# Attention made tile by tile: q, k and v of 128 tokens in one group of split fp32 products, used and dropped

## The reference, cut to what matters

```python
q = apply_rope(rmsnorm((x @ Wq + bq).heads, qn_w), pos)          # 16 heads of 128
w = softmax((x @ Wcmp + bcmp) in groups of 4 tokens)
entries = weighted sum of each 4 tokens                            # 512 entries
ck = apply_rope(rmsnorm(entries @ Wk + bk, kn_w), block_ends)
cv = entries @ Wv + bv
sc = where(causal, q @ ck.T / sqrt(128), NEG)
tv, ti = top_k(sc, 8)                                              # 8 entries of 512
ctx_sparse = softmax over those 8 of cv
lk = apply_rope(rmsnorm((x @ Wlk + blk).heads, kn_w), pos)
lv = (x @ Wlv + blv).heads
ctx_local = softmax(q @ lk.T / sqrt(128)) @ lv                    # own and former 128 tokens
out = ((ctx_sparse + ctx_local) / 2).heads_joined @ Wo + bo
x = layernorm(x + out)                                             # then the experts
```

## Time and profile before

| | us |
|---|---|
| median of 3 runs (lowest, highest) | 2773.98 (2771.32, 2775.93) |
| span of the profiled execution, first to last instruction | 2770.1 |
| its PE busy / DVE / ACT / POOL | 2483.0 / 1509.1 / 915.2 / 897.2 |
| preparation (`compress`) | 0 to 60 |
| heads | 60 to 1770 |
| first norm, routing, experts, second norm | 1770 to 2770 |

### The profile page before, as it was taken

One profiled execution on the slowest core, in us unless ns is written; L12 is line 12 of the kernel. 1 busy time (PEld: TensorE's weight loads), 2 busy tenths in 40 slices (PEclk: granted clock), 3 DMA queues, 4 the chain that ended last, 5 costly groups with the idle time before them and its releaser, 6 DMA issues. The chain is left out here.

```text
span 2770.1 us, 43311 instructions
## 1 busy us (share of the span) xinstructions
PE 2483.0 (90%) x14112; PEld 1983.1 (72%) x14113; DVE 1509.1 (54%) x4673; ACT 915.2 (33%) x2231; POOL 897.2 (32%) x969
## 2 busy tenths in 40 slices
PE   6999999999999999999999998599278999988873
PEld 4676876876876876877877877377167999877852
DVE  5566666666666666666666666707023222344357
ACT  2143343343343343343333334332012333333331
POOL 1333233233233233233233232224702110256256
PEclk9999999999999999999999999789688999999986
DMA  4900000000000000000000000101514332446446
GB/s 183 356 1 21 13 1 21 14 1 21 14 1 21 14 1 21 14 1 21 14 1 21 1 1 1 68 0 46 197 44 147 110 112 76 141 161 218 133 132 187
DMA packets 63673, 176.74 MB, mean 64 GB/s; under 512 B 8832, under 2 KB 10368, under 8 KB 63232
## 3 DMA queue, kind: packets, MB, share of 16 engines
q1 hardware_dynamic: 31792, 84.39, 8.7%
q0 software_dynamic: 19456, 69.22, 7.7%
q10 hardware_dynamic: 12240, 20.73, 2.0%
HBM read 107.20 MB, written 67.11 MB: 63 GB/s over the span
## 5 line engine op out<-in xcount | busy, mean ns | idle before, releaser
L448 PE MATMUL bank<-xT,wh 128*128 128x512 f32 x1024 | 468.5, 601 | 1.6 <-PEq L156 1.6
L698 POOL TENSOR_TENSOR prob<-prob,share 128x256 f32<-128x256 f32 (+1 forms) x256 | 153.6, 600 | 818.5 <-DVE share L611 818.5
L448 PEld LDWEIGHTS bank<-xT,wh 128*128 128x128 f32 x1024 | 187.8, 194 | 190.7 <-issue 190.7
L1389 POOL TENSOR_TENSOR ring_lo<-staged,ring_hi 128x1088 fp32r<-128x1088 f32 x51 | 127.9, 2523 | 475.9 <-ACT ring_hi L1348 475.4
L646 ACT COPY probT<-bank 128x128 f32<-128x128 f32 (+3 forms) x256 | 109.1, 426 | 482.2 <-PE bank L490 482.2
L455 PE MATMUL bank<-wh,xT 128*128 128x128 f32 x2048 | 263.4, 275 | 0.0
L606 DVE SCALAR_TENSOR_TENSOR prob<-taken,prob 128x32 f32<-128x32 f32 (+15 forms) x256 | 113.2, 442 | 250.9 <-ACT prob L657 250.9
L455 PEld LDWEIGHTS bank<-wh,xT 128*128 128x128 f32 x2048 | 248.8, 192 | 0.0
L900 PE MATMUL bank<-ring_hi,xslo 128*128 128x352 f32 x600 | 205.1, 342 | 47.3 <-issue 27.7
L501 PEld LDWEIGHTS bank<-probT,cv 128*128 128x128 f32 x1280 | 178.4, 192 | 43.4 <-issue 30.1
L556 DVE SCALAR_TENSOR_TENSOR turned<-bank,wh,sin 32x512 f32<-32x512 f32 x128 | 95.0, 742 | 192.7 <-ACT square L640 192.6
(11 more groups left out here) (274 smaller groups left out, 5621.2 us busy)
## 6 DMA issues: line engine op xcount, KB each, us to landing
staged<-in_wexp POOLq DMA_DIRECT2D x64, 544.0 KB, 5.1
slots_in<-wo SPq DMA_DIRECT2D x41, 512.0 KB, 6.0
xslot<-slots_in SPq DMA_DIRECT2D x76, 256.0 KB, 2.6
slots_out<-yslot ACTq DMA_DIRECT2D x76, 256.0 KB, 2.0
wh<-in_wh SPq DMA_DIRECT2D x16, 833.0 KB, 4.6
slots_out<-wo SPq DMA_DIRECT2D x9, 512.0 KB, 6.2
staged_shared<-in_wexp SPq DMA_DIRECT2D x8, 544.0 KB, 7.0
staged<-in_wexp SPq DMA_DIRECT2D x8, 544.0 KB, 8.4
```

The source lines that it names most:

```text
L448: mm = pe.matmul(dst[:, :], weight(par, which, k), xT[:, k, chunk(c)], start=(k == 0), stop=(k == KC - 1))
L698: pool.tensor_tensor(pl, pl, share[b][:, 1:2].to_broadcast(list(pl.shape)), ALU.mult)
L1389: pool.tensor_tensor(wlo[:, e % RING, quarter(q)], staged[e % 2][:, quarter(q)], whi[:, e % RING, quarter(q)].bitcast(F32), ALU.subtract). ...
```

## The change

**In the heads.** There are no units any more. In step n PE makes q, k and v of tile n+2 together (`pe_qkv`): tokens on partitions, 384 columns (q, k, v) per product, four chunks of channels, three split products each, so 12 parts of 128x384 into one PSUM bank. DVE adds the bias of q and k (`nat`), ACT copies v into a ring of eight tiles and squares q and k with a running sum (two instructions of 128x129), POOL rotates (`pool_rope`: two multiplies and an add, 128x128, 128x256 and 128x128) and takes the power -1/2 of two columns (`pool_rstd`). In the next step DVE scales the key (`dve_scale_keys`), PE turns q and k (`pe_qkT`, two transposes), and ACT copies both to `qkT`. Scores of tile n+1 read that copy in the following step. Turning probabilities and the context come two steps after the scores instead of one, the output product three steps after, and the addition to `acc` four. The output of a tile is now made and added to `acc` for every head (three parts, 256 additions) instead of once for two heads (six parts, 128 additions). The value bias is added on ACT and DVE to the context. Scores have two PSUM banks.

**Weights.** A head's weights are split once in a high and a low part, in four pieces during the head before: ACT converts (`act_weights`), POOL subtracts (`pool_weights`). SP loads the next head's weights when the low parts are made. The zeroing of the slots in memory is issued half before and half after the loads for heads 2 and 3.

**In the preparation.** x is split: ACT copies the high part of each turned piece and DVE subtracts for the low part. The rotation tables are made with tokens on partitions: POOL loads cos and sin in four rounds of 512 tokens, scales them by the norm weights and takes every fourth column for the entries; PE turns 12 squares a round, and ACT copies four pieces a round. All four rounds share one buffer, so a round begins when PE has turned the last. DVE rotates `ckT` after the fourth. A load of 16x128x2 single biases and small loads of the biases of a head (128 elements each) are new.

```diff
-    def pe_unit(pe, h, par, u, of_kind):
-
-        n = h * 16 + u
-        dst = b_unit[u % 2]
-        if u == 0:
-            pe.wait_ge(w_in[par], of_kind * 16 + 16)
-        wait_for(pe, s_uvec, n - 1)
-        if u < 8:
-            which, c = (1, u) if u < 4 else (0, u - 4)
-            for k in range(KC):
-                mm = pe.matmul(dst[:, :], weight(par, which, k), xT[:, k, chunk(c)],
-                               start=(k == 0), stop=(k == KC - 1))
...
+    def pe_qkv(pe, a):
+        if a.tile == 0:
+            pe.wait_ge(w_low, (a.head + 1) * KC)
+        wait_for(pe, s_nat, a.n)
+        wait_for(pe, s_v, a.n)
+        cols = slice(a.tile * P, (a.tile + 1) * P)
+        for k in range(KC):
+            mm = three_products(pe, b_qkv[:, 0:3 * D], (xhi[:, k, cols], xlo[:, k, cols]),
+                                (whi[a.par][:, k, :], wlo[a.par][:, k, :]), k == 0, k == KC - 1)
+        mm.then_inc(s_qkv, 1)
+
+    def pe_qkT(pe, a):
+        pe.wait_ge(s_scaled, a.n + 1)
+        wait_for(pe, s_probT, a.n - 2)
+        for g in range(2):
+            mm = pe.transpose(b_qkT[:, g * P:(g + 1) * P], roped[:, a.two, g, :], ident[:, :])
+        mm.then_inc(s_qkT, 1)
...
+    def pe_pair(pe, i, **ends):
+        for at in steps(i, **ends):
+            for off, stage in ((0, pe_scores), (-2, pe_turn), (2, pe_qkv), (1, pe_qkT), (-2, pe_context), (-3, pe_out)):
+                if at(off).live:
+                    stage(pe, at(off))
...
+    def dve_scale_keys(dve, a):
+        dve.wait_ge(s_rope, a.n + 1)
+        dve.wait_ge(s_rstd, a.n + 1)
+        keys = roped[:, a.two, 1, :]
+        dve.tensor_scalar(keys, keys, rstd[:, a.slot, 1:2], None, ALU.mult).then_inc(s_scaled, 1)
...
+        dve.wait_ge(s_qkv, a.n + 1)
+        dve.tensor_tensor(nat[:, a.two, :, 0:P], b_qkv[:, 0:2 * D].rearrange("p (g d) -> p g d", g=2),
+                          bqk[:, a.par, :].rearrange("p (g d) -> p g d", g=2), ALU.add).then_inc(s_nat, 1)
...
+    def dve_pair(dve, i, **ends):
+        for at in steps(i, **ends):
+            for off, stage in ((-4, dve_acc), (-3, dve_ctx), (0, dve_select), (1, dve_scale_keys), (2, dve_nat),
+                               (0, dve_keep)):
+                if at(off).live:
+                    stage(dve, at(off))
...
+    def act_v(act, a):
+        act.wait_ge(s_nat, a.n + 1)
+        act.copy(v[:, a.j % VKEEP, :], b_qkv[:, 2 * D:3 * D]).then_inc(s_v, 1)
+
+    def act_squares(act, a):
+        if not isinstance(a.n, int) or a.n > 1:
+            act.wait_ge(s_rstd, a.n - 1)
+        for g, factor in ((0, 1.0), (1, D ** -0.5)):
+            act.activation(junk[:, a.two, g, 0:P + 1], nat[:, a.two, g, 0:P + 1], ACT.Square, scale=factor,
+                           accum_out=ssq[:, a.slot, g:g + 1]).then_inc(s_sq, 1)
...
+    def act_pair(act, i, **ends):
+        for at in steps(i, **ends):
+            for off, stage in ((-3, act_ctx), (-2, act_probT), (0, act_exp), (1, act_qkT), (2, act_v), (2, act_squares)):
+                if at(off).live:
+                    stage(act, at(off))
...
+    def pool_rope(pool, a):
+        table = rope[:, a.tile, :]
+        cos = table[:, 0:2 * P].rearrange("p (g d) -> p g d", g=2)
+        sin = table[:, 2 * P:3 * P].rearrange("p (g d) -> p g d", g=2)[:, ::-1, :]
+        pool.wait_ge(s_nat, a.n + 1)
+        wait_for(pool, s_qkT, a.n - 1)
+        pool.tensor_tensor(cross[:, :, :], nat[:, a.two, :, 0:2 * ROT], sin, ALU.mult).then_inc(s_mult, 1)
+        pool.tensor_tensor(roped[:, a.two, :, :], nat[:, a.two, :, 0:P], cos, ALU.mult).then_inc(s_mult, 1)
+        pool.wait_ge(s_mult, a.n * 2 + 2)
+        part = roped[:, a.two, :, 0:2 * ROT].rearrange("p g (s d) -> p g s d", s=2)
+        swapped = cross[:, :, :].rearrange("p g (s d) -> p g s d", s=2)[:, :, ::-1, :]
+        pool.tensor_tensor(part, part, swapped, ALU.add).then_inc(s_rope, 1)
+
+    def pool_rstd(pool, a):
+        pool.wait_ge(s_sq, a.n * 2 + 2)
+        pool.tensor_tensor(rstd[:, a.slot, :], ssq[:, a.slot, :], half[:, :], ALU.pow).then_inc(s_rstd, 1)
...
+            def tables(c):
+                cols = slice(c * CH, (c + 1) * CH)
+                if c:
+                    pool.wait_ge(tab_turn, c * TPC)
+                pool.dma_start(cosq[:, :], t["cos"][:, cols]).then_inc(cos_in, 16)
+                pool.dma_start(sin[:, :], t["sin"][:, cols]).then_inc(sin_in, 16)
...
+            for c in range(1, NCH):
+                tables(c)
```

More of the change, by code:

```diff
@@ L335, in _ @@
[L335 to L350 removed]
+            dve.wait_ge(vproj, 1)
@@ L362, in heads @@
-    nfac = [sb(f"nfac{i}", [P, NT]) for i in range(2)]
-    top = [sb(f"top{i}", [P, TOPK + 1]) for i in range(2)]
-    nbias = [sb(f"nbias{i}", [P, 2]) for i in range(2)]
-    total = [sb(f"total{i}", [P, 2]) for i in range(2)]
-    share = [sb(f"share{i}", [P, 2]) for i in range(2)]
+    nat = sb("nat", [P, 2, 2, P + 2])
+    junk = sb("junk", [P, 2, 2, P + 2], BF16)
+    cross = sb("cross", [P, 2, 2 * ROT])
+    roped = sb("roped", [P, 2, 2, P])
+    qkT = sb("qkT", [P, 2, KEEP, P])
+    v = sb("v", [P, VKEEP, D])
@@ L367, in heads @@
+    ssq = sb("ssq", [P, KEEP, 2])
+    rstd = sb("rstd", [P, KEEP, 2])
+    half = sb("half", [P, 2])
+    top = sb("top", [P, KEEP, TOPK + 1])
+    lifted = sb("lifted", [P, 2])
+    nbias = sb("nbias", [P, KEEP, 2])
+    total = sb("total", [P, KEEP, 2])
+    share = sb("share", [P, KEEP, 2])
     taken = sb("taken", [P, C])
-    prob = [sb(f"prob{i}", [P, C + 2 * P]) for i in range(2)]
+    prob = sb("prob", [P, KEEP, C + 2 * P])
     probT = sb("probT", [P, C + 2 * P])
-    even_hi = sb("even_hi", [P, S], F32R)
@@ L482, in pe_turn, with __init__ @@
-    def pe_turn(pe, n, tile):
-        pe.wait_ge(s_prob, n + 1)
-        wait_for(pe, s_probT, n)
-        pr = prob[tile % 2]
-        for b in range(blocks(tile)):
+    class At:
+        def __init__(self, i, j, first, last):
+            self.live = not (first and j < 0) and not (last and j >= STEPS)
+            self.n = i * STEPS + j
+            self.head = i * 2 + j // NT
+            self.pair = i + j // STEPS
+            self.par = j // NT % 2
+            self.tile = j % NT
+            self.slot = j % KEEP
+            self.two = j % 2
+            self.j = j
@@ new lines, in steps, with pe_scores @@
+    def steps(i, first=False, last=False):
+        for j in range(-2 if first else 0, STEPS + (4 if last else 0)):
+            yield lambda off, j=j: At(i, j + off, first, last)
+    def pe_scores(pe, a):
+        n, tile, w = a.n, a.tile, width(a.tile)
+        q = qkT[:, 0, a.slot, :]
+        wait_for(pe, s_taken, n)
+        wait_for(pe, s_exp, n - 1)
+        pe.wait_ge(s_qkTc, n + 1)
+        if tile % KEEP:
+            pe.matmul(b_local[:, 0:2 * P], q, qkT[:, 1, a.slot - 1:a.slot + 1, :].rearrange("p s d -> p (s d)"),
+                           start=True, stop=True)
+        else:
+            if tile:
+                pe.matmul(b_local[:, 0:P], q, qkT[:, 1, KEEP - 1, :], start=True, stop=True)
+            pe.matmul(b_local[:, P:2 * P], q, qkT[:, 1, 0, :], start=True, stop=True)
+        dst = b_score[a.two]
+        pe.matmul(dst[:, 0:w], q, ckT[:, 0:w], start=True, stop=False)
+        pe.matmul(dst[:, w - EPT:w], identb[:, :], diag[:, :], start=False, stop=True).then_inc(s_sc, 1)
@@ new lines, in dve_pair, with act_ctx @@
+    def dve_pair(dve, i, **ends):
[4 more added lines that the diff above has]
+                    stage(dve, at(off))
+            a = at(0)
+            if a.live and at(NT).live and a.tile == WO_AT + 1:
+                dve_wo(dve, a.head + 1, 1 - a.par)
+    def act_ctx(act, a):
+        if a.tile == 0:
+            act.wait_ge(blv_in[a.par], (a.pair + 1) * 16)
+        act.wait_ge(s_ctx, a.n + 1)
+        wait_for(act, s_out, a.n - 1)
+        act.activation(chi[:, a.two, :], b_ctx[:, 0:P], ACT.Identity, bias=blv[:, a.par:a.par + 1]).then_inc(s_ctxh, 1)
```

714 lines of the change are left out of this document (329 added, 385 removed).

## The result

| | before | changed |
|---|---|---|
| median of the runs, us | 2772.65 (2770.31 to 2775.93, 4 runs) | 2543.91 (2542.74 to 2545.38, 4 runs) |
| profiled span | 2770.1 | 2540.9 |
| preparation | 60 | 113.5 |
| from there to the first selection | 57.1 | 13.9 |
| 255 steps between first and last selection | 1644.7 | 1402.3 |

The ratio is 0.917, with an interval of 0.916 to 0.919: 8% faster, where 6% was forecast. The four stretches give +53.5 - 43.2 - 242.4 + 2.9 = -229.2 us of span.

What follows compares the result with a forecast made beforehand. The prediction took the heads to be bound by the columns PE streams. From a span of 2770.1 us, heads -163, lead -42, end +2 and preparation +36 gave 2603, so a median of 2607 us, 6% faster; range 2525 to 2695.

Steps and rivals of the forecast that it cites:

- the pace of the selections: Sign of a right forecast in the heads: selection instructions 5.7 to 5.9 us apart on the mean, against 6.45 before.
- Prices on PE: Costs per product from record starts: fp32 unit 3.43 us, its squares 0.81, split part of 384 columns 0.174 by interpolation.
- rival 1: Heads: parts run at the 352-column pace (-43 us) and half the old wait gaps go (-40): 2525 us; chance 0.12.
- What stays is 56.0 us per head: Heads: scores, turned probabilities, context, output and all gaps remain on PE; with 37.0 added, 93.0 us a head, -163 us.
- The lead -42, the end +2: Before the first selection 57.1 us of head 0 units become 15, -42; one more step of delay at the end, +2.
- The preparation +36: Block ahead of the heads ends at about 96 us instead of 60, with three table rounds of 8.3; bounds +25 to +55.
- The bias load costs nothing: Preparation: POOL's load of 4096 single bias values in 8-byte pairs is in time for PE; costed at nothing.
- SP's zeroing costs nothing: Heads: head 2's weights queue behind 20 zeroing transfers, some 40 us, but are needed two heads later; costed at nothing.
- The other engines: Heads, per step: DVE 3.8 us, ACT 4.7 at most, POOL 3.4, all below PE's 5.81.
- rival 3: Heads: POOL's new passes and power are dearer and POOL becomes the bound, 7.0 us a step: 2910 us; chance 0.05.
- The cover is 0.4 us per step: Turns of q and k: DVE's chain from output to scaled key takes 3.1 us, PE's work meanwhile 3.5, so no wait.
- Rival 2: Heads: DVE's half grows by 0.7 us, PE waits 0.3 a step at the turns of q and k: 2684 us; chance 0.22.

## Why the prediction was nearly right, and which steps failed

The range and the sign held; the forecast was 63 us too high. That the range held was in part luck: with the preparation as forecast, the time would have been 2526, at the lower bound of 2525. Of the signs that it named, the pace of the selections missed (5.50 for 5.7 to 5.9), and the others came: parts 0.176 apart, heads beginning at 113.5, a full clock, 1.6 us of waits before L560. By its own steps:

- **"The heads are bound by the number of columns that PE streams."** Right before and after: 1390.74 busy of 1402.3.
- **Prices on PE.** A part was put at 0.174 and is 0.176. The Trainium skill's rule (TensorE: Matmul & The Clock Gate, Back-to-back issue gap), 162 ns at 384 columns, doesn't hold for these parts; the line through the two measured widths did. So the half of rival 1 that rested on it fell.
- **"What stays is 56.0 us per head"** is the step that failed. That number carried all gaps of the kernel before, "I take no stall in the sum" notwithstanding. Of the steps 50.5 us stay, the new work is 37.4, and the head is 88.0: nothing of the 5.5 of gaps stayed. (The 50.5 is written there without its terms; the starts on PE in the 14 heads between first and last give 50.7.) It makes 255/16 x 5.0 = 80 us, -242 instead of -163. That is the other half of rival 1, "the gaps go, too", which got half weight in a case with a chance of 0.12. The runs give the cause of that in part: in the kernel before the distance is worth 2.1 us a head in the middle and 10.5 in the last, in the changed one 0.11 a step; the new form of the scores comes with 1.5 a head, and about 1 stays open. "Gaps" was also too narrow a name, since PE was idle for only some 2 us a head before. A sum of 50.5 stood in the prediction's own text; with it, the heads come out at 87.5.
- **"The lead -42, the end +2."** -43.2 and +2.9.
- **"The preparation +36"**, measured +53.5, at the far bound of +55. x was all turned at 56.6, as forecast at 56. Behind that the power was put at 1 us and took 6.30, and each round at 8.3 and took about 12.9. In the rounds "five POOL instructions, say 3" was 5.5 (three of 1.56 each, two of 0.4); the loads were 1.2 of issue and 3.3 until they landed, 4.5 for "say 4"; and between POOL's last pass and its next load lie 3.2 for "12 turns, 1.3", since the turns ran 0.21 apart at a granted clock of 0.50 (83.7 to 86.6), where 0.11 was read at the full clock. The block also ends behind the fourth round's turns and ACT's copies, not with DVE's rotation.
- **"The bias load costs nothing", "SP's zeroing costs nothing".** x was all turned when the sum had it, so the bias load took nothing that shows, and no wait for weights is among PE's in the heads. Nothing was tried on either.
- **"The median lies 3.9 above the profiled span."** In the changed kernel's own profiled execution 1.8 us lie around the span (2542.74 - 2540.9), so 2 us of the 63 are here.
- **The other engines.** Per step DVE 3.8 (945/255 = 3.7), ACT 4.7 at most (3.4), POOL 3.4 (3.6). POOL is at 66% in the heads, and rival 3 had no ground: its power took 0.71, not 1.0 or more, its rotation 0.58 + 0.71 + 0.46 for 0.34 + 0.61 + 0.34.
- **"The cover is 0.4 us per step"** at the turns of q and k. Right in place and nearly in size: a step 0.30 shorter brings the wait. Rival 2 did not come, since nothing in DVE's half was dearer than put.

The two errors had opposite signs: -79 in the heads, +17.5 in the preparation.

## What to carry to other kernels

When work is taken out of a bound stage, sum what stays from its single steps, and put the gaps of the old schedule beside it as a term of its own with a chance of its own: if the change also lengthens the distance between an engine's step and the one that waits for it, part of the gaps goes with it. Before a stage is moved ahead of the bound loop, look at the engine that runs it alone there: rounds of load, pass and turn through one shared buffer cost their latencies, and one wide round on DVE gave 1.5% here. And an order on one engine can't be changed for the sake of one wait without reading what the engine behind it, which works in its written order, has queued: the unit ahead of the turns cost 8%.

## What the runs showed of the hardware that I had not expected

- POOL's one-operation pass over 128x512 with a scalar per partition takes 1.56 us, the same with a second operation 0.69. The kernel before has the two-operation form in its heads, so its rows didn't warn.
- POOL and DVE stand still for one another when both read two operands from SBUF: POOL's power takes 6.30 us beside DVE's addition and 1.05 without it, one low part 6.24 for 0.99, and each ends 0.9 us behind the addition. The Trainium skill (GPSIMD Engine Reference, Specifications) names the shared interface and two SBUF inputs of DVE as the case; the traces agree, with these numbers for the price. It goes the other way too: DVE's addition takes 10.29 us where its first 4.9 lie beside POOL's own bias addition, and 6.21 and 6.29 us beside low parts alone; a DVE pass of 64x512 beside POOL's bias addition takes 4.82 for 0.68. In the kernel before it was 8.83, with 3.5 us beside POOL's.
- The chips differ by 2% on the kernel before (2772.65 on the first, 2718 to 2723 on the two others) and on the changed one (2543.91 and 2494.66), while the step of the heads is the same to 0.01 us. In the changed kernel the difference lies behind the heads, 1011.2 against 959.9 us. So comparisons across chips need the stretch or the ratio.
